# Two convolutions and a spline layer on one core: mask rows laid out channel by channel, the steps' chain moved to GpSimd, one load issued ahead of a store

## The chip, the cores and the metric

The kernel runs on one core of one Trainium2 chip. The metric is the device time of a launch in microseconds; of several runs the median is taken. PE is TensorE, ACT is ScalarE, DVE is VectorE, POOL is GpSimd and SP is SyncE, whose queue issues most of the DMAs.

## The reference

`x` is float32 [32, 64, 56, 56] (32 images, 64 channels). The first block is two 3x3 convolutions, weights reduced to their signs, each followed by a batch norm over images and pixels, a relu between them, and a residual sum. The second block is a spline per channel.

```python
w1b = sign(w1); w2b = sign(w2)
out = relu(_batchnorm(_conv3x3(x, w1b), gamma1, beta1))
out = _batchnorm(_conv3x3(out, w2b), gamma2, beta2)
x   = relu(out + x)
...
x_aff = clip(x * a + b, -CLAMP, CLAMP)
u = (x_aff + 1.0) * 0.5 * (K - 1)
i = floor(u); t = clip(u - i, 0, 1)
spline = alpha_table[i0] * b0 + alpha_table[i1] * b1 + alpha_table[i2] * b2 + alpha_table[i3] * b3
y_nl = einsum('bchwr,cr->bchw', spline, mix)
return id_gain * x + y_nl + bias
```

`K` is 32 knots, `alpha_table` is [32, 8], `mix` is [64, 8], and `b0` to `b3` are the cubic basis functions of `t`.

## The kernel before, in words

**Three stages.** The first convolution reads the 32 images as 16 pairs (128 partitions: 2 images of 64 channels) and stores its result in a scratch tensor; the second reads that, with batch norm and relu applied on the way in, and stores to a second scratch tensor; the spline stage reads that, adds `x`, and works through 32 chunks of 128 x 1568 values. Pairs are counted over both convolutions: 0 to 15 in the first, 16 to 31 in the second.

**A pair of a convolution.** SP loads it (L273 in a loop, L294 for the first two pairs of the second convolution, each of those with two small halo DMAs). In the second convolution ACT normalises it in place (L381) and writes its high part as fp16 (L399); the pair that opens the convolution goes in pieces (L365, L374). DVE normalises the halo (L480 to L492) and writes the low part (L509). PE multiplies all taps, both parts, 288 products in four tiles (L741). ACT evacuates each half (L420), DVE takes statistics (L547), SP stores (L279). Each engine runs its own list in order; the lists are written in rounds of two pairs, with the first and the last round of each convolution written out apart. Where the first convolution ends, SP's list is: store of pair 14, load and halo of pair 16, store of pair 15, load and halo of pair 17 (L288 to L296).

**The tables.** In the first convolution's first round PE multiplies `alpha` with three arrangements of `mix` (L720): as it is, and for each half of the channels repeated for four groups (`mix_by_group`, filled by eight small DMAs, L240). DVE scales the result and makes 17 centres' coefficients of five tables (`coefficients`, L572). In the second convolution's first round DVE forms the differences between neighbouring centres, picks for each partition those of its group and splits them into a high and a low part (`steps`, L599 to L619). GpSimd then writes 80 diagonal weight tiles of 128 x 32 from them (L349), which PE uses only in the spline stage.

**A chunk of the spline stage.** Each channel's value at a pixel has a cell number. Sixteen DMAs (`spread`, L938) copy the chunk's cells into `cell4`, so that four rows of partitions hold the same channel; row `g` of the four is compared with thresholds of its own. Before, those rows are `g * 32 + channel`. Comparing gives four masks: two "middle" masks by DVE (L1161, `middle`) and two "edge" masks by ACT (L1058). PE multiplies the masks with the diagonals into one of two PSUM buffers by turns (L1303), table by table: NEAR and FAR with all four masks, middle ones first, then SQ, LIN and VAL with the edge masks alone; SQ also takes a product that adds the near part (L1313). DVE reads each table: `near_cube` (L1181), `far_cube` (L1188), `square` (L1202), `slope` (L1210), `value` (L1223), and does `far_part` (L1195), `add_slope` (L1216), `finish` (L1230), `offsets` (L1154), `fixed` (L1146), `linear` (L1140) between. A table may be begun when the one two before it has been read. The order on DVE is written by hand (L1276 to L1294). A middle mask of the next chunk may be written when PE has done with the one of this chunk, which is after FAR's middle products; it waits for the whole FAR table (L1160).

The chunk that opens the stage spreads its cells by products with an identity, whose 32 columns are taken four times (L1327), instead of DMAs.

```python
def middle(c, q):
    dve.wait_ge(copied[c % 2], copies(c))
    dve.wait_ge(table_ready, used(c - 1, T_FAR))
...
def table(c, t):
    wait_past(pe, table_used, used(c, t) - 2)
```

## Time and profile before

| what | value |
|---|---|
| median of 3 runs | 1140.85 us (1138.58 to 1143.94) |
| profiled execution, its own time | 1139.08 us |
| its span | 1137.2 us, mean granted clock 0.989 |
| PE busy | 1081.0 us (95%) |
| DVE busy | 966.2 us (85%) |
| ACT busy | 899.3 us (79%) |
| POOL busy | 137.5 us (12%) |
| DMA | 259.46 MB, mean 228 GB/s |

The first convolution lasts until about 204 us of the span, the second until about 411, the spline stage until the end. Busy time is the time in which an engine executes; the difference to the span is idle time, and it only matters on the engine that the others wait for.

### The profile page before, as it was taken

Reading aid. Unit: us, or ns where it says so; the run is one execution under the profiler, and the core shown is the slowest. Engines: PE = TensorE matmul, PEld = TensorE weight load, DVE = VectorE, ACT = ScalarE, POOL = GpSimd, SP = SyncE. Lnnn points to the kernel's source line nnn. Section 1 sums busy time; section 2 is a strip of 40 time slices with the busy share of each in tenths; the row PEclk is TensorE's granted clock in tenths of the full one; section 3 lists DMA queues with packets and bytes.
Section 4 is the critical chain, followed back from the end, with each engine's and each line's share of the span. In section 5 each row is a group of like instructions: output and inputs, shape, how many; then the busy total and the mean of one; then the engine's idle time right before and its main releaser. Section 6 shows DMA issues by size and latency. Waiting matters only on the chain.

```text
span 1137.2 us, 53175 instructions
## 1 busy us (share of the span) xinstructions
PE 1081.0 (95%) x24650; PEld 724.2 (64%) x24650; DVE 966.2 (85%) x959; ACT 899.3 (79%) x410; POOL 137.5 (12%) x195
## 2 busy tenths in 40 slices
PE   6999999699999968999999999999999999999996
PEld 5777777577777745556656656656666556656564
DVE  5856656687767779999999999999999998999997
ACT  4445443767777648999999999999999999999971
POOL 6000000058100000101101011011110110101100
PEclk9999999899999989999999999999999999999999
DMA  8677674677677936799898989989989988998652
GB/s 288 221 293 285 251 278 175 224 248 298 263 284 291 349 164 161 185 233 225 228 234 213 237 203 234 222 220 235 228 209 235 226 225 212 233 233 200 165 131 87
DMA packets 57465, 259.46 MB, mean 228 GB/s; under 512 B 16080, under 2 KB 16080, under 8 KB 49232
## 3 DMA queue, kind: packets, MB, share of 16 engines
q1 hardware_dynamic: 48496, 208.40, 54.6%
q0 software_dynamic: 8640, 48.17, 23.2%
q8 instruction: 148, 2.42, 0.9%
q10 hardware_dynamic: 160, 0.30, 0.1%
q14 instruction: 21, 0.17, 0.0%
HBM read 104.29 MB, written 77.07 MB: 159 GB/s over the span
## 4 chain that ended last, share of the span: by engine, by line
PE 86%; DVE 7%; issue 3%; DMA 1%; ACT 1%; SPq 0%; DVEq 0%; ACTq 0%
PE tab L1303 49%; PE acc L741 30%; PE tab L1313 7%; DVE middle_mask L1161 1%; DMA halo<-y_scratch 1%; DVE far_sq L1210 1%; DMA w_raw<-in_w 1%; ACT xin L381 1%; ACT yout L420 1%; DVE poly L1202 0%; DVE far L1188 0%; DVE stats L547 0%; DVE offset L1154 0%; DVE poly L1216 0%; DVE band_split L509 0%
## 5 line engine op out<-in xcount | busy, mean ns | idle before, releaser
L1303 PE MATMUL tab<-edge_mask,diag 128*32 128x392 bf16 x10240 | 446.6, 329 | 5.8 <-issue 2.5
L1303 PEld LDWEIGHTS tab<-edge_mask,diag 128*32 128x32 f16 x10240 | 283.5, 97 | 160.6 <-issue 20.1
L1058 ACT ACTIVATE edge_mask<-cell,thr 128x6272 bf16<-128x6272 bf16 x62 | 338.6, 5509 | 2.0 <-DMA cell<-cell 2.0
L420 ACT ACTIVATE yout<-acc 128x1568 f32<-128x1568 f32 x64 | 94.5, 1477 | 167.5 <-PE acc L741 146.9
L741 PE MATMUL acc<-band_split,w 64*64 64x385 f16 (+2 forms) x4608 | 194.6, 329 | 9.9 <-DVE band_split L509 4.9
L741 PE MATMUL acc<-split,w 64*64 64x385 f16 (+3 forms) x4608 | 191.5, 326 | 11.2 <-DVE w L468 10.0
L1303 PE MATMUL tab<-middle_mask,diag 128*32 128x392 bf16 x4096 | 187.2, 329 | 7.5 <-issue 5.5
L547 DVE BATCH_NORM_STATS2 stats<-yout 128x392 f32 (+1 forms) x240 | 117.9, 555 | 89.1 <-ACT yout L420 89.1
L741 PEld LDWEIGHTS acc<-band_split,w 64*64 64x64 f16 x4608 | 150.0, 109 | 54.3 <-issue 8.8
L741 PEld LDWEIGHTS acc<-split,w 64*64 64x64 f16 x4608 | 144.7, 108 | 57.1 <-issue 11.9
L1303 PEld LDWEIGHTS tab<-middle_mask,diag 128*32 128x32 f16 x4096 | 110.6, 97 | 72.6 <-DVE middle_mask L1161 10.4
L1161 DVE TENSOR_SCALAR middle_mask<-cell,thr 128x6272 bf16<-128x6272 bf16 x62 | 114.5, 1846 | 0.0
L973 POOL DMA_DIRECT2D lin<-far x32 | 50.2, 1568 | 497.7 <-DVE far L1195 497.7
L1313 PE MATMUL tab<-poly,ident 128*32 128x392 f32 x1024 | 92.4, 493 | 1.3 <-issue 1.3
L1188 DVE SCALAR_TENSOR_TENSOR far<-tab,first,far 128x1568 f32<-128x1568 f32 x31 | 57.4, 1851 | 25.6 <-PE tab L1303 25.6
L520 DVE SCALAR_TENSOR_TENSOR split<-split,xin 128x3136 f16<-128x3136 f16 (+4 forms) x19 | 55.0, 2908 | 10.1 <-ACT split L410 9.8
L1033 ACT ACTIVATE poly<-offset 128x1568 f32<-128x1568 int32 x32 | 48.4, 1511 | 18.6 <-DVE offset L1154 16.9
L1313 PEld LDWEIGHTS tab<-poly,ident 128*32 128x32 f32 x1024 | 34.1, 110 | 43.6 <-issue 38.7
L1202 DVE SCALAR_TENSOR_TENSOR poly<-tab,first,dist_sq 128x1568 f32<-128x1568 f32 x31 | 57.3, 1847 | 4.1 <-PE tab L1313 4.1
L1181 DVE SCALAR_TENSOR_TENSOR poly<-tab,first,poly 128x1568 f32<-128x1568 f32 x31 | 57.2, 1846 | 4.0 <-PE tab L1303 4.0
L1195 DVE SCALAR_TENSOR_TENSOR far<-far,cst,far_sq 128x1568 f32<-128x1568 f32 x32 | 59.3, 1852 | 1.2
L1210 DVE SCALAR_TENSOR_TENSOR far_sq<-tab,first,offset 128x1568 f32<-128x1568 f32 x31 | 57.2, 1846 | 0.9 <-PE tab L1303 0.8
(140 smaller groups left out, 962.0 us busy)
## 6 DMA issues: line engine op xcount, KB each, us to landing
y_scratch<-yout SPq DMA_DIRECT2D x32, 1568.0 KB, 6.2
cell<-cell SPq DMA_DIRECT2D x496, 98.0 KB, 4.6
xin<-y_scratch SPq DMA_DIRECT2D x16, 1568.0 KB, 6.2
lin<-far POOLq DMA_DIRECT2D x32, 784.0 KB, 8.6
out<-lin SPq DMA_DIRECT2D x31, 784.0 KB, 5.3
xin<-in_x SPq DMA_DIRECT2D x15, 1568.0 KB, 6.5
lin<-y_scratch SPq DMA_DIRECT2D x30, 784.0 KB, 9.3
lin<-in_x POOLq DMA_DIRECT2D x28, 784.0 KB, 7.9
```

The source lines that it names most:

```text
L420: act.activation(yout[b][:, :].rearrange("p (r k x) -> p k r x", r=2, k=TILES)[:, 2 * part:2 * part + 2], acc[:, 4 * part:4 * part + 4, 0: ...
L547: dve.bn_stats(stats[:, bass.ds(COUNTS * (g - base) + t, 1), :], yout[b][:, own]).then_inc(counted, 1)
L741: mm = pe.matmul(to[:, top:end, cols], weights[part][own, tap * C:(tap + 1) * C], image[own, first + dy + top:first + dy + end, from_cols] ...
L1058: act.activation(mask_of(c, q)[:, :, :], cell4[c % 2][:, :, :], ACT.Sign, bias=thr[:, q:q + 1]).then_inc(sign_mask_ready, 1)
L1161: dve.tensor_scalar(mask_of(c, q)[:, :, :], cell4[c % 2][:, :, :], thr[:, q:q + 1], None, ALU.is_ge).then_inc(mask_ready, 1)
L1181: dve.scalar_tensor_tensor(out=quarters(poly[c % 2]), in0=summed(c, T_NEAR), scalar=base(c, T_NEAR), in1=quarters(poly[c % 2]), op0=ALU.ad ...
L1188: dve.scalar_tensor_tensor(out=quarters(far[c % 2]), in0=summed(c, T_FAR), scalar=base(c, T_FAR), in1=quarters(far[c % 2]), op0=ALU.add, o ...
L1195: dve.scalar_tensor_tensor(out=far[c % 2][:, :], in0=far[c % 2][:, :], scalar=cc(AMP), in1=far_sq[:, :], op0=ALU.mult, op1=ALU.mult).then_ ...
L1202: dve.scalar_tensor_tensor(out=quarters(poly[c % 2]), in0=summed(c, T_SQ), scalar=base(c, T_SQ), in1=quarters(dist_sq), op0=ALU.add, op1=A ...
L1210: dve.scalar_tensor_tensor(out=quarters(far_sq), in0=summed(c, T_LIN), scalar=base(c, T_LIN), in1=quarters(offset[c % 2]), op0=ALU.add, op ...
L1303: mm = pe.matmul(tab[(c + t) % 2][j * GROUP:(j + 1) * GROUP, sub, 0:SUB], keep["diag"][part][:, j % 2, t, q, :], mask_of(c, q)[:, j, sub * ...
L1313: mm = pe.matmul(tab[(c + T_SQ) % 2][j * GROUP:(j + 1) * GROUP, sub, 0:SUB], keep["ident"][:, j * GROUP:(j + 1) * GROUP], poly[c % 2][:, s ...
```

## The change

1. SP no longer issues the eight DMAs that fill `mix_by_group`; GpSimd fills it by eight copies, and PE waits for them before the tables.
2. Where the first convolution ends, the last store (pair 15) goes behind the load and halo of pair 17.
3. `steps` runs on GpSimd, after `coefficients`, by instructions that treat all 128 partitions alike (of_group selects the own row). The five last instructions of `coefficients` no longer wait for one another. Nothing of `steps` remains in DVE's list.
4. The four rows of a channel are now `4 * channel + g` (copies, diagonals' identity, thresholds, `mix_by_group`).
5. The opening chunk's cells are spread by 16 products of 128 x 128 weights instead of 64 with 32 columns each; the weights lie in the memory of `dist_sq`.
6. DVE's middle masks stand earlier in the chunk: the first behind `finish`, the second behind `far_part`. They wait for FAR's last middle product instead of the whole FAR table.

```diff
-                for g in range(4):
-                    sp.dma_start(mix_by_group[:, half, g * GROUP:(g + 1) * GROUP],
-                                 mix_t[:, half * GROUP:(half + 1) * GROUP]).then_inc(small_loaded, 16)
...
-                    if b == 0 and is_last(n):
-                        store(2 * i + 1, 1)
+                if is_last(n):
+                    store(2 * i + 1, 1)
...
+            def fold(t, width):
+
+                while width > 1:
+                    width //= 2
+                    link(pool.tensor_tensor(t[:, 0:width], t[:, 0:width], t[:, width:2 * width], ALU.add))
+
+            def steps():
+
+                for l in range(3):
+                    link(pool.tensor_tensor(step[:, l, :, :], coef[:, l, :, 1:CENTRES], coef[:, l, :, 0:STEPS],
+                                            ALU.subtract))
+                    signed = step[:, l, :, 0:STEPS:2]
+                    link(pool.tensor_scalar(signed, signed, 0.5, None, ALU.mult))
+                link(pool.tensor_tensor(halves[:, :, :], step[:, 0, :, 0:STEPS // 2:2], step[:, 0, :, STEPS // 2:STEPS:2],
+                                        ALU.add))
+                for width in (2, 1):
+                    link(pool.tensor_tensor(halves[:, :, 0:width], halves[:, :, 0:width], halves[:, :, width:2 * width],
+                                            ALU.add))
+                link(pool.tensor_copy(keep["plain"][:, :], coef[:, 0, :, 0]))
+                link(pool.tensor_tensor(keep["first"][:, :], keep["plain"][:, :], halves[:, :, 0], ALU.add))
+                for half in range(2):
+                    for odd, quads in enumerate((EDGE_QUADS, MIDDLE_QUADS)):
+                        to = dsel[:, half, :, quads[0]:quads[1] + 1]
+                        for g in range(4):
+                            frm = step[:, 1 + half, :, 2 * g + odd:STEPS:8]
+                            if g == 0:
+                                link(pool.tensor_scalar(to, frm, of_group[:, g:g + 1], None, ALU.mult))
+                            else:
+                                link(pool.tensor_scalar(own_step[:, :, :], frm, of_group[:, g:g + 1], None, ALU.mult))
+                                link(pool.tensor_tensor(to, to, own_step[:, :, :], ALU.add))
+                link(pool.tensor_copy(dhi16[:, :, :, :], dsel[:, :, :, :]))
+                link(pool.tensor_copy(dhi[:, :, :, :], dhi16[:, :, :, :]))
+                link(pool.tensor_tensor(dlo[:, :, :, :], dsel[:, :, :, :], dhi[:, :, :, :], ALU.subtract))
...
+            link(pool.memset(keep["spread"][:, :, :], 0.0))
+            link(pool.affine_select(out=keep["spread"][:, :, :], in_=keep["spread"][:, :, :], compare_op=ALU.not_equal,
+                                    fill=1.0, base=0, pattern=[[-1, P], [0, 4]], channel_multiplier=1))
             link(pool.memset(ident4[:, :], 0.0))
...
-                                        base=-g * GROUP, pattern=[[-1, GROUP]], channel_multiplier=1))
+                                        base=-g, pattern=[[-4, GROUP]], channel_multiplier=1))
+            link(pool.memset(turn4[:, :], 0.0))
+            for g in range(1, 4):
+                link(pool.affine_select(out=turn4[:, :], in_=turn4[:, :], compare_op=ALU.not_equal, fill=4.0 * g,
+                                        base=-g, pattern=[[-4, GROUP]], channel_multiplier=1))
+            fold(turn4, GROUP)
+            for q in range(QUADS):
+                lowest = SHIFT + 2 * (step_at(q, 0) + 1)
+                link(pool.tensor_scalar(keep["above"][:, q:q + 1], turn, lowest, None, ALU.add))
+                if q in EDGE_QUADS:
+                    link(pool.tensor_scalar(thr[:, q:q + 1], turn, -1.0, 0.5 - lowest, ALU.mult, ALU.add))
+                else:
+                    link(pool.tensor_scalar(thr[:, q:q + 1], turn, lowest, None, ALU.add))
+            for g in range(4):
+                link(pool.tensor_scalar(of_group[:, g:g + 1], turn, 4.0 * g, None, ALU.is_equal))
...
+            pool.wait_ge(small_loaded, 5 * 16)
+            for half in range(2):
                 for g in range(4):
-                    above = SHIFT + 2 * (step_at(q, g) + 1)
-                    link(pool.memset(thr[g * GROUP:(g + 1) * GROUP, q:q + 1],
-                                     0.5 - above if q in EDGE_QUADS else above))
-                    link(pool.memset(keep["above"][g * GROUP:(g + 1) * GROUP, q:q + 1], above))
-
+                    pool.tensor_copy(mix_by_group[:, half, g:P:4],
+                                     mix_sb[:, half * GROUP:(half + 1) * GROUP]).then_inc(mix_spread, 1)
...
-            pool.wait_ge(steps_ready, 1)
+            pool.wait_ge(coefficients_ready, TABLES)
+            steps()
...
-                    link(dve.tensor_scalar(coef[:, :, t, :], coef[:, :, t, :], f, None, ALU.mult), chain)
-
-            def steps():
...
+                    dve.tensor_scalar(coef[:, :, t, :], coef[:, :, t, :], f, None,
+                                      ALU.mult).then_inc(coefficients_ready, 1)
...
-                    if n == half_rounds:
-                        steps()
...
-                pe.wait_ge(small_loaded, 13 * 16)
+                pe.wait_ge(small_loaded, 5 * 16)
+                pe.wait_ge(mix_spread, 8)
...
-                        sp.dma_start(cell4[c % 2][g * GROUP:(g + 1) * GROUP, j, :],
+                        sp.dma_start(cell4[c % 2][g:P:4, j, :],
...
-                dve.wait_ge(table_ready, used(c - 1, T_FAR))
+                dve.wait_ge(middle_used, c)
...
                 finish(c - 1)
+                if c + 1 < CHUNKS:
+                    middle(c + 1, MIDDLE_QUADS[0])
                 far_cube(c)
                 far_part(c)
                 if c + 1 < CHUNKS:
-                    middle(c + 1, MIDDLE_QUADS[0])
+                    middle(c + 1, MIDDLE_QUADS[1])
                 square(c)
                 if c + 1 < CHUNKS:
                     offsets(c + 1)
                 slope(c)
-                if c + 1 < CHUNKS:
-                    middle(c + 1, MIDDLE_QUADS[1])
                 add_slope(c)
...
-                ones = keep["ident"][:, :].bitcast(BF16)
                 for j in (2 * s, 2 * s + 1):
                     for u in range(2):
-                        for g in range(4):
-                            mm = pe.matmul(tab[s][g * GROUP:(g + 1) * GROUP, 2 * (j % 2) + u, 0:SUB],
-                                           ones[:, 2 * GROUP * j + 1:2 * GROUP * (j + 1):2],
-                                           cell[0][:, (2 * h + u) * SUB:(2 * h + u + 1) * SUB], start=True, stop=True)
+                        mm = pe.matmul(tab[s][:, 2 * (j % 2) + u, 0:SUB],
+                                       keep["spread"][:, j * GROUP:(j + 1) * GROUP, :],
+                                       cell[0][:, (2 * h + u) * SUB:(2 * h + u + 1) * SUB], start=True, stop=True)
...
+                    if t == T_FAR and q == MIDDLE_QUADS[-1]:
+                        mm.then_inc(middle_used, 1)
...
+            "dist_sq": sb("dist_sq", [P, CHUNK]),
...
+        keep["spread"] = keep["dist_sq"][:, 0:2 * P].bitcast(BF16).rearrange("p (k g) -> p k g", g=4)
```

SP's queue at the end of the first convolution, before. The two stores that stand first (x2) are those of pairs 13 and 14; `xin` and `halo` are the loads of a pair and its halo.

```order
L221 REGISTER_ALU
L221 COMPARE_AND_BRANCH
L279 DMA y_scratch<-yout 128x3136 x2
L294 DMA xin<-y_scratch 128x3136
L294 DMA halo<-y_scratch 64x2x56 x2
L279 DMA y_scratch<-yout 128x3136
L294 DMA xin<-y_scratch 128x3136
L294 DMA halo<-y_scratch 64x2x56 x2
L273 DMA xin<-y_scratch 128x3136
```

And now:

```order
L226 REGISTER_ALU
L226 COMPARE_AND_BRANCH
L281 DMA y_scratch<-yout 128x3136 x2
L296 DMA xin<-y_scratch 128x3136
L296 DMA halo<-y_scratch 64x2x56 x2
L296 DMA xin<-y_scratch 128x3136
L296 DMA halo<-y_scratch 64x2x56 x2
L281 DMA y_scratch<-yout 128x3136
L275 DMA xin<-y_scratch 128x3136
```

The store of pair 15 moved behind the load of pair 17 and its halo.

DVE's list in a chunk of the spline stage, before (L1161 are the middle masks, L1188 `far_cube`, L1202 `square`, L1210 `slope`):

```order
L1181 SCALAR_TENSOR_TENSOR poly<-tab,first,poly 128x1568
L1230 SCALAR_TENSOR_TENSOR lin<-poly,cst,lin 128x1568
L1188 SCALAR_TENSOR_TENSOR far<-tab,first,far 128x1568
L1195 SCALAR_TENSOR_TENSOR far<-far,cst,far_sq 128x1568
L1161 TENSOR_SCALAR middle_mask<-cell,thr 128x6272
L1202 SCALAR_TENSOR_TENSOR poly<-tab,first,dist_sq 128x1568
L1154 TENSOR_SCALAR offset<-zbuf 128x1568
L1210 SCALAR_TENSOR_TENSOR far_sq<-tab,first,offset 128x1568
L1161 TENSOR_SCALAR middle_mask<-cell,thr 128x6272
L1216 SCALAR_TENSOR_TENSOR poly<-far_sq,poly 128x1568
```

And now (L1192 are the masks, L1219 `far_cube`, L1233 `square`, L1241 `slope`):

```order
L1212 SCALAR_TENSOR_TENSOR poly<-tab,first,poly 128x1568
L1261 SCALAR_TENSOR_TENSOR lin<-poly,cst,lin 128x1568
L1192 TENSOR_SCALAR middle_mask<-cell,thr 128x6272
L1219 SCALAR_TENSOR_TENSOR far<-tab,first,far 128x1568
L1226 SCALAR_TENSOR_TENSOR far<-far,cst,far_sq 128x1568
L1192 TENSOR_SCALAR middle_mask<-cell,thr 128x6272
L1233 SCALAR_TENSOR_TENSOR poly<-tab,first,dist_sq 128x1568
L1185 TENSOR_SCALAR offset<-zbuf 128x1568
L1241 SCALAR_TENSOR_TENSOR far_sq<-tab,first,offset 128x1568
L1247 SCALAR_TENSOR_TENSOR poly<-far_sq,poly 128x1568
```

The first mask moved from behind `far_part` to ahead of `far_cube`, the second from behind `slope` to ahead of `square`.

## Rows read from the trace of the kernel before

**Rows 1.** Busy time per engine in two stretches: us, count, clock, DMA share, GB/s.

```profile
250.00:380.00 130.00, 128.93 (x3134) 97.25 (x3130) 96.92 (x177) 92.85 (x44) 34.03 (x59) 1.00 0.75 283
...
500.00:700.00 200.00, 196.55 (x4382) 123.10 (x4386) 188.91 (x119) 194.71 (x85) 23.17 (x19) 1.00 0.90 225
```

**Rows 2.** Timeline, opening of the second convolution: start, length, [idle before <- releaser].

```profile
195.41 1.39 SPq L294 DMA_DIRECT2D halo<-y_scratch  x1
...
206.39 0.38 SPq L294 DMA_DIRECT2D xin<-y_scratch  x1
...
217.64 3.00 ACT L381 ACTIVATE xin<-xin,cst 128x3136 f32<-128x3136 f32 x1 [2.47 <-DMA halo<-y_scratch]
...
223.58 3.50 DVE L509 SCALAR_TENSOR_TENSOR band_split<-band_split,xin 128x1568 f16<-128x1568 f16 x2 [4.32 <-ACT band_split L399]
...
227.18 13.79 PE L741 MATMUL acc<-band_split,w 64*64 64x392 f16 x288 [3.37 <-DVE band_split L509]
```

**Rows 3.** Windows of one us: PE, PEld, DVE, ACT, POOL, granted clock, DMA.

```profile
228.00:229.00 1.00, 1.00 (x21) 0.85 (x16) 0.96 (x3) 1.00 (x1) 0.00 (x0) 0.50 1.05 201
...
241.00:242.00 1.00, 0.00 (x0) 0.00 (x0) 1.00 (x1) 0.97 (x1) 1.00 (x1) 1.00 0.00 0
```

**Rows 4.** Timeline, two evacuations one pair apart in the first convolution.

```profile
179.72 1.48 ACT L420 ACTIVATE yout<-acc 128x1568 f32<-128x1568 f32 x1 [4.50 <-PE acc L741]
...
191.54 1.48 ACT L420 ACTIVATE yout<-acc 128x1568 f32<-128x1568 f32 x1 [4.42 <-PE acc L741]
```

**Rows 5.** Timeline around the steps' chain in the second convolution's first round.

```profile
231.09 0.23 DVE L602 TENSOR_TENSOR step<-coef 128x80 f32<-128x80 f32 x1
...
237.07 0.38 POOL L349 TENSOR_SCALAR diag<-ident,dhi 128x32 f16<-128x32 f32 x1 [210.44 <-DVE dlo L618]
...
238.67 3.54 DVE L509 SCALAR_TENSOR_TENSOR band_split<-band_split,xin 128x1568 f16<-128x1568 f16 x2
239.04 3.32 POOL L349 TENSOR_SCALAR diag<-ident,dhi 128x32 f16<-128x32 f32 x1
...
242.47 2.85 PE L741 MATMUL acc<-band_split,w 64*64 64x392 f16 x65 [1.50 <-DVE band_split L509]
```

**Rows 6.** Timeline, a quiet chunk of the spline stage, DVE and PE.

```profile
900.48 1.85 DVE L1188 SCALAR_TENSOR_TENSOR far<-tab,first,far 128x1568 f32<-128x1568 f32 x1 [0.53 <-PE tab L1303]
...
904.14 1.85 DVE L1161 TENSOR_SCALAR middle_mask<-cell,thr 128x6272 bf16<-128x6272 bf16 x1
...
908.54 1.84 DVE L1210 SCALAR_TENSOR_TENSOR far_sq<-tab,first,offset 128x1568 f32<-128x1568 f32 x1
...
910.30 1.84 DVE L1161 TENSOR_SCALAR middle_mask<-cell,thr 128x6272 bf16<-128x6272 bf16 x1
...
910.78 2.93 PE L1303 MATMUL tab<-middle_mask,diag 128*32 128x392 bf16 x64
...
913.54 2.83 PE L1303 MATMUL tab<-edge_mask,diag 128*32 128x392 bf16 x64
...
917.66 1.85 DVE L1181 SCALAR_TENSOR_TENSOR poly<-tab,first,poly 128x1568 f32<-128x1568 f32 x1
...
921.80 1.85 DVE L1188 SCALAR_TENSOR_TENSOR far<-tab,first,far 128x1568 f32<-128x1568 f32 x1 [0.53 <-PE tab L1303]
```

**Rows 7.** Waits of the whole span: us in total, times, longest.

```profile
PE acc L741 <- DVE split L520: 0.5, 1, 0.5
```

**Rows 8.** Timeline of PE from chunk 1 to chunk 2.

```profile
472.13 2.84 PE L1303 MATMUL tab<-edge_mask,diag 128*32 128x392 bf16 x64 [0.81 <-DVE poly L1202]
...
476.54 1.51 PE L1303 MATMUL tab<-middle_mask,diag 128*32 128x392 bf16 x32 [0.24 <-DVE middle_mask L1161]
```

**Rows 9.** DMA view: the cell copies (us to landing), and queue 1 in 429 to 441.

```profile
cell<-cell SPq DMA_DIRECT2D x496, 98.0 KB, 4.6
...
q1 hardware_dynamic: 700, 1.49, 54.2%
```

**Rows 10.** Waits in 480 to 1100 us.

```profile
PE tab L1303 <- issue: 8.0, 7, 2.1
```

32 lines of the change are left out of this document (9 added, 23 removed).

## The prediction

> **What bounds the kernel now.** I read the page's engine totals first (PE is busy 95% of the span), then the windows by stage, the chain of waits for the places where PE stands still, and the timeline around each. In the late part of the second convolution PE is busy 128.93 of 130 us, and in the spline stage 196.55 of 200, beside DVE at 188.91 and ACT at 194.71 [rows 1]. So PE sets the time nearly everywhere, and a change pays only where PE waits. There are three such places that this change touches.
>
> The first is the opening of the second convolution. The load of its second pair (image data of pair 17, counted over both convolutions, and its halo) is issued at 206.39, behind the first convolution's last store [rows 2]. ACT starts to normalise that pair at 217.64, after 2.47 us of waiting for the halo, so it was free at 215.17; DVE's split follows at 223.58, and PE, done with the first pair, stands still for 3.37 us until 227.18 [rows 2]. What follows costs more: after that idle time the granted clock is 0.50 (1.2 GHz) in 228 to 229 [rows 3]. That pair takes PE 13.79 us, where a pair at full clock takes 191.54 - 179.72 = 11.82, read from the distance of two evacuations in the first convolution [rows 2, 4]. A pair later PE waits 1.50 us more, for DVE's split, which began at 238.67 because the steps' chain stood ahead of it, from 231.09 until GpSimd's first diagonal could start at 237.07 [rows 5]; inside that gap of 1.50 us the clock is at 1.00 (2.4 GHz) [rows 3], and no slower stretch follows it.
>
> The second is the change of chunk in the spline stage. In a quiet stretch a chunk lasts 21.32 us (far_cube at 921.80 has one 21.32 before it, at 900.48, and so have the others). The second middle mask starts at 910.30 and ends at 912.14; PE's 64 products with middle masks are busy for 2.93 us from 910.78, the 64 with edge masks after them, from 913.54, for 2.83 [rows 6]. So 0.10 to 0.11 us is lost in a chunk: 2.76 from start to start, where 2.65 would do.
>
> The third is small: a wait of 0.5 us for DVE's split behind the coefficients [rows 7].
>
> **The change part by part.** *The load ahead of the store.* Before, the first pair's halo DMAs are issued from 195.41 for 1.39, so SP is free at 196.80, and its next wait (lo_done) had long been met. The load of pair 17 will go out there, 9.6 us earlier. Today its halo lands by 217.64, 11.2 us after that issue; as long a flight from 196.8 ends at 208, before ACT's 215.17. ACT's two passes, 2.47 us earlier, let DVE start at 223.58 - 2.47 = 221.11, and PE at 227.18 - 2.45 = 224.73, after a gap of 0.92. **Gain 2.45 us.** A gap of 1.50 us did not lower the clock and one of 3.37 did; 0.92 lies below both, so I take the clock as kept, and the pair as 11.82 instead of 13.79: **gain 1.97 us**, with bounds of 0 (the clock falls all the same) and 1.97. The store goes out when it does now, since it waits for ACT's last evacuation; the loads behind it wait for DVE's splits of pair 16, much later. The load queues behind the first pair's load on the same queue, so that one isn't delayed.
>
> *The steps' chain on GpSimd.* DVE loses its chain between the statistics and the next halo, 231.09 to about 237.0, 5.9 us. The split of pair 18, ready today at 238.67 + 3.54 = 242.21, is then ready at 236.3 at the latest. PE will want it at 224.73 + 11.82 = 236.55. **Gain 1.50 us**; bounds 1.50 and, if the split comes a microsecond later, 0.7. On GpSimd the chain is 42 instructions, and 80 for the diagonals as before. A diagonal took 0.38 us [rows 5]; with a link of 0.1 (an estimate) 122 x 0.48 = 59 us, twice that if DVE holds it up. It starts in the first convolution's second round, and PE reads the diagonals in the spline stage, over 25 pairs of 11.8 us later; only if that cover of 300 us were gone would it cost. The diagonal at 239.04 took 3.32 us beside DVE's split, while the two splits together took 3.54, against 3.50 in the pair before [rows 2, 5], so GpSimd was what waited [rows 5]; I cost DVE nothing. The Trainium skill (SBUF — State Buffer, Who interferes with whom) says more: a DVE instruction with two SBUF inputs and a GpSimd one that reads SBUF exclude each other, and the first to start wins, so DVE can lose too. By that rule each of the first convolution's splits could start up to one short GpSimd instruction late; the row agrees for one side only, and the sum would stay the same, since PE isn't waiting for DVE there.
>
> *Coefficients without links.* Five instructions no longer wait for one another; I take 0.3 of the 0.5 us wait [rows 7]. **Gain 0.3 us**, bounds 0 and 0.5.
>
> *Masks earlier on DVE.* Of a chunk's 21.32 us DVE is idle only 0.53, before far_cube [rows 6], so its work is 20.79. PE without its loss needs 21.32 - 0.11 = 21.21, in eight pieces of about 2.65 (NEAR and FAR two each, SQ one and the one that adds the near part, LIN and VAL one each). With both masks where the diff puts them, DVE's one wait per chunk moves to near_cube, 0.30 after NEAR's last product: 5.6 us into the chunk. Steps from the rows: near_cube to far_cube 4.14 less 0.53 idle = 3.6, far_cube (900.48) to mask (904.14) 3.66, mask to slope 4.40 of which the mask 1.76 [rows 6]. So the first mask starts at 5.6 + 3.6 = 9.2 (PE has released the buffer at 7.95), far_cube at 11.0, the second mask at 14.6, square at 16.4 and ends at 18.25, slope at 19.05 and ends at 20.9. PE wants square at 18.55 and slope at 21.2: 0.3 us of slack at either, and the masks are over 4 us early. **Gain 0.11 x 29 chunks = 3.2 us.** But in chunk 1, where DVE is still behind, the second mask now stands before square. There PE's VAL started at 472.13 and the wait for the mask ended at 476.54 [rows 8]. Now VAL starts 1.76 later, at 473.9, NEAR at 473.9 + 2.65 = 476.55 without a mask wait, and its second half, which before started at 476.54, at 477.88: **loss 1.3 us**. Net 1.9; bounds 3.2 and, if the slack of 0.3 proves 0.1 short, -1.
>
> *Rows channel by channel.* Copies, diagonals and thresholds keep number and size; only the destination's partitions are every fourth. The copies take 4.6 us to land [rows 9]. They are issued in the chunk before their use, and no engine waits for them in the chunk shown. I cost this at nothing, either way. The Trainium skill (SBUF — State Buffer, Door 1: The DMA port swizzle) says that 32 neighbouring partitions reach half of the DMA ports; partitions four apart reach all of them on the write side, the read side is unchanged. By that rule the copies get no slower, perhaps faster, which no wait would turn into time.
>
> *The rest.* 16 products of 128 rows replace 64 in column groups of 32 that ran four abreast: the same time within 0.3 us. Eight small DMAs go, and eight GpSimd copies must be done before PE builds the tables behind the second pair's first tile, over 11.8 us after PE began; GpSimd's opening grows by a few short operations. I call it covered; without cover it is a microsecond or two.
>
> **Sum:** 2.45 + 1.97 + 1.50 + 0.3 + 1.9 = 8.1 us. The profiled execution took 1139.08 us, which makes 1131.0. The median of the three runs, 1140.85, is 1.8 above it, so I say 1132.7.
>
> **The rivals.** *A. The clock falls or the second gap comes back* (chance 0.14). For it: 0.92 us is worked out from other engines' times, and pair 18's split has only 0.25 us of slack. Then 8.1 - 1.97 - 1.5 = 4.6, time 1136.2. Against: both gaps shrink by amounts that rows give.
>
> *B. DVE's new order costs what it gains or more* (0.13). DVE is busy 188.91 of 200 us. If square or slope come 0.1 us too late in each chunk, 3 us go and the start's 1.3 remain: gain 8.1 - 3.2 - 3 = 1.9, time 1139. Against: the one idle of 0.53 [rows 6].
>
> *C. The copies get slower* (0.07), the case on the other side. The DMA engines are busy 0.90 of the spline stage [rows 1]. In 429 to 441, with the copies nearly alone, they hold 54.2% of 12 us = 6.5 us in which they moved 1.49 MB [rows 9], so a chunk's 1.57 MB cost 6.9 us of its 0.90 x 21.3 = 19.2. From a copy time 1.3 times today's the engines are full and each chunk waits; at 1.5 times a chunk takes 19.2 + 3.4 = 22.6 us, 1.4 more, over 30 chunks 42 us: 1175. Against: each partition's run is the same 3136 bytes.
>
> *D. PE's unexplained pauses* (within all cases): in the spline stage it stands still for 8.0 us, seven times, with nothing to wait for [rows 10]. They may fall otherwise, by 2 or 3 us.
>
> **How the numbers follow.** My forecast has 0.66: 1132.7, itself within 1128 and 1136. A measurement of this kernel can tell about 0.5%, 5.7 us, from no change, so faster is below 1135.1. Forecast: most of it faster; A and B mostly the same; C slower, with a little of B. Faster 0.67, same 0.24, slower 0.09. The range leaves out C and the tails: 1127 to 1140.
>
> **What would show it.** In the changed profile: the pair-17 load issued near 197, no ACT wait for a halo at 217, PE's gap near 224 under 1 us, the clock at 1.00 from 216 on, the next gap gone, the second convolution's end about 6 us earlier; no wait of the weight load for middle masks, DVE's idle time ahead of near_cube instead of far_cube, and chunks of 21.21 us. Wrong would be: the clock at 0.50 near 228, PE waiting for square or slope, masks or ACT waiting for copies, or an idle PE at 26 us.

## The result and the profile after

The changed kernel took 1126.34 us (median, 1123.17 to 1131.16) against 1139.11 for the kernel before: ratio 0.9883, 95% interval 0.985 to 0.9916, so 12.8 us or 1.2% faster. Three repeats beside the experiments gave 0.99, 0.988 and 0.9896, gains of 11.7, 12.6 and 10.9 us. One execution among all runs, of the kernel b_steps below, took 1919.33 us and is left out of its numbers. I had forecast 1132.7 us, a gain of 8.1, and a range that began at 1127: the direction and most places were right, the size too small.

The profiled execution took 1126.34 us, its span 1124.5, 12.7 less than before. First the opening of the second convolution, in the timeline of the changed kernel (start, length, engine and line, in brackets the idle time before and what ended it):

```profile
197.69 0.87 SPq L296 DMA_DIRECT2D xin<-y_scratch  x1
...
210.72 14.30 PE L771 MATMUL acc<-band_split,w 64*64 64x392 f16 x288 [3.61 <-DVE band_split L540]
...
216.17 2.99 ACT L433 ACTIVATE xin<-xin,cst 128x3136 f32<-128x3136 f32 x1
...
222.10 3.49 DVE L561 SCALAR_TENSOR_TENSOR band_split<-band_split,xin 128x1568 f16<-128x1568 f16 x2 [2.39 <-ACT band_split L451]
...
225.70 30.32 PE L771 MATMUL acc<-band_split,w 64*64 64x392 f16 x728 [0.68 <-issue]
...
233.94 3.49 DVE L561 SCALAR_TENSOR_TENSOR band_split<-band_split,xin 128x1568 f16<-128x1568 f16 x2
```

The load of pair 17 goes out at 197.69 instead of 206.39 [rows 2], ACT normalises that pair without a wait, and PE stands still for 0.68 us instead of 3.37. From 225.70 it then works through 30.32 us: the gap of 1.50 us before pair 18 [rows 5] is gone, since DVE's split of that pair starts at 233.94. The windows (busy us of PE, PEld, DVE, ACT and POOL, granted clock, DMA share, GB/s) show the clock, and the later stretch of [rows 1]:

```profile
500.00:700.00 200.00, 199.13 (x4513) 133.85 (x4505) 195.19 (x122) 198.38 (x84) 24.74 (x18) 1.00 0.88 229
228.00:229.00 1.00, 1.00 (x32) 0.83 (x25) 0.00 (x0) 1.00 (x2) 0.00 (x0) 1.00 0.94 401
```

The clock stays at 1.00 in 228 to 229, where it was 0.50 [rows 3]. In 500 to 700 PE stands still for 0.87 us instead of 3.45, at a DMA share of 0.88 instead of 0.90. How long the second convolution lasts is read from the start of its first pair to the matmul that averages the statistics behind it. In the kernel before, the PE timeline has them at

```profile
209.63 14.18 PE L741 MATMUL acc<-band_split,w 64*64 64x392 f16 x288 [3.60 <-DVE band_split L488]
...
412.87 0.38 PE L813 MATMUL acc<-mv,avg 128*128 128x2 f32 x2 [2.33 <-DVE mv L656]
```

and in the changed one the second of them at

```profile
408.63 0.38 PE L843 MATMUL acc<-mv,avg 128*128 128x2 f32 x2 [2.33 <-DVE mv L687]
```

so 412.87 - 209.63 = 203.24 us have become 408.63 - 210.72 = 197.91. The start itself lies 1.1 us later than before (210.72 against 209.63); in the eighteen traces it lies anywhere from 209.6 to 212.3, for the kernel before and its variants too, so this is not put down to the change.

GpSimd now makes the steps in the first convolution, from the same timeline:

```profile
45.90 3.42 POOL L324 TENSOR_TENSOR step<-coef 128x80 f32<-128x80 f32 x1 [16.19 <-DVE coef L649]
...
54.45 3.33 POOL L344 TENSOR_TENSOR dsel<-dsel,own_step 128x10 f32<-128x10 f32 x1
...
70.47 0.38 POOL L401 TENSOR_SCALAR diag<-ident,dhi 128x32 f16<-128x32 f32 x1
```

Its chain takes 24.6 us, most links 0.2 to 0.35 us and three over 3.3. Here is a quiet chunk (one in which PE never waits), DVE and PE:

```profile
1029.79 2.84 PE L1334 MATMUL tab<-middle_mask,diag 128*32 128x392 bf16 x64
...
1035.40 1.85 DVE L1212 SCALAR_TENSOR_TENSOR poly<-tab,first,poly 128x1568 f32<-128x1568 f32 x1 [0.27 <-PE tab L1334]
...
1038.93 1.85 DVE L1192 TENSOR_SCALAR middle_mask<-cell,thr 128x6272 bf16<-128x6272 bf16 x1
1040.70 1.85 DVE L1219 SCALAR_TENSOR_TENSOR far<-tab,first,far 128x1568 f32<-128x1568 f32 x1
...
1044.36 1.85 DVE L1192 TENSOR_SCALAR middle_mask<-cell,thr 128x6272 bf16<-128x6272 bf16 x1
...
1046.12 1.85 DVE L1233 SCALAR_TENSOR_TENSOR poly<-tab,first,dist_sq 128x1568 f32<-128x1568 f32 x1
...
1048.77 1.85 DVE L1241 SCALAR_TENSOR_TENSOR far_sq<-tab,first,offset 128x1568 f32<-128x1568 f32 x1
...
1050.99 2.32 PE L1334 MATMUL tab<-middle_mask,diag 128*32 128x392 bf16 x49
```

The next chunk's masks are done well ahead, DVE's one wait stands at near_cube, and the chunk lasts 1050.99 - 1029.79 = 21.20 us, where it was 21.32 [rows 6]. Chunk 1 pays for it:

```profile
465.94 1.85 DVE L1192 TENSOR_SCALAR middle_mask<-cell,thr 128x6272 bf16<-128x6272 bf16 x1
467.71 1.85 DVE L1233 SCALAR_TENSOR_TENSOR poly<-tab,first,dist_sq 128x1568 f32<-128x1568 f32 x1
...
469.61 2.84 PE L1334 MATMUL tab<-edge_mask,diag 128*32 128x392 bf16 x64 [2.57 <-DVE poly L1233]
...
476.85 1.84 PE L1334 MATMUL tab<-edge_mask,diag 128*32 128x392 bf16 x40 [0.75 <-issue]
```

The second mask stands before square, and PE waits 2.57 us for square (0.81 before [rows 8]). Here the clock stayed at 1.00 behind that wait. It did not always: nine traces have this wait of 2.57 us, and in five of them (again, again2, old_rows, old_rows2 and few_copies, described below) the clock was at 0.50 (1.2 GHz) for about 3 us behind it, as in the first repeat:

```profile
468.41 4.37 PE L1334 MATMUL tab<-edge_mask,diag 128*32 128x392 bf16 x64 [2.57 <-DVE poly L1233]
```

```profile
469.00:470.00 1.00, 1.00 (x16) 0.49 (x12) 1.00 (x2) 1.00 (x1) 0.00 (x0) 0.50 0.92 185
```

From the near part's add in chunk 1 to that in chunk 2 it is 22.63 us before, 24.0 to 24.9 where the clock held, and 25.5 where it fell. Last the waits and the DMA view of the changed kernel: PE's waits for nothing in 500 to 1100 (in total, times, longest), the copies of the cells (KB, us to landing), and queue 1 in 425 to 437, where the first copies run nearly alone (packets, MB, share):

```profile
PE tab L1334 <- issue: 3.5, 6, 1.2
```

```profile
cell<-cell SPq DMA_DIRECT2D x496, 98.0 KB, 4.0
...
q1 hardware_dynamic: 704, 1.49, 47.6%
```

PE's pauses "<- issue" fell from 8.0 us [rows 10] to 3.5. The copies land after 4.0 us instead of 4.6, and for 1.49 MB they hold the DMA engines for 0.476 x 12 = 5.7 us instead of 6.5 [rows 9].

From here on a measure is used that every trace gives: the distance between the starts of the add of the near part (the 32 matmuls tab<-poly,ident) in chunk 2 and in chunk 31, less 29 times a quiet chunk. It is what PE's **pauses** cost in 29 chunks, with the rare wait beside them and the slower clock behind some of them. Before, 488.49 to 1120.07 is 631.58 us, less 29 x 21.31 leaves 13.6. After, 486.46 to 1107.37 is 620.91, less 29 x 21.20 leaves 6.1. So of the 12.7 us of span, 5.3 come from the second convolution, 3.2 from the quiet chunks and 7.5 from shorter pauses; 2.3 are lost in chunk 1 (0.75 of them a pause) and 1.1 ahead of the second convolution. The 7.5 were not in the forecast.

### The profile page after: what moved, and what is told of

It reads as the page before. It is cut to its first block, busy times and chain, and to the rows that moved or that the text cites. A ratio compares the mean times of both kernels' runs of the same rounds, so it can differ in the third digit from the quotient of the medians.

```text
span 1124.5 us, 53088 instructions
## 1 busy us (share of the span) xinstructions
PE 1074.4 (96%) x24602; PEld 751.0 (67%) x24602; DVE 963.5 (86%) x931; ACT 899.2 (80%) x410; POOL 170.2 (15%) x236
## 4 chain that ended last, share of the span: by engine, by line
PE 94%; DVE 3%; issue 1%; DMA 1%; ACT 0%; ACTq 0%; DVEq 0%
PE tab L1334 52%; PE acc L771 34%; PE tab L1344 8%; DMA w_raw<-in_w 1%; DVE middle_mask L1192 0%; DVE far_sq L1241 0%; PE tab L1356 0%; DVE poly L1233 0%; DVE lin L1276 0%; DVE poly L1272 0%; DVE middle_mask L1201 0%; DVE stats L581 0%; ACT zbuf L1044 0%; DVE edge_mask L1201 0%; DVE offset L1185 0%
## 5 line engine op out<-in xcount | busy, mean ns | idle before, releaser
L1334 PE MATMUL tab<-edge_mask,diag 128*32 128x392 bf16 x10240 | 453.0, 329 | 9.7 <-issue 4.3
L1334 PEld LDWEIGHTS tab<-edge_mask,diag 128*32 128x32 f16 x10240 | 297.5, 97 | 153.5 <-issue 16.3
L771 PE MATMUL acc<-split,w 64*64 64x385 f16 (+3 forms) x4608 | 192.2, 327 | 11.5 <-DVE w L520 10.3
L771 PE MATMUL acc<-band_split,w 64*64 64x385 f16 (+3 forms) x4608 | 192.7, 327 | 6.5 <-DVE band_split L540 3.6
L771 PEld LDWEIGHTS acc<-split,w 64*64 64x64 f16 x4608 | 143.9, 108 | 59.0 <-issue 12.8
L1334 PEld LDWEIGHTS tab<-middle_mask,diag 128*32 128x32 f16 x4096 | 119.2, 97 | 56.7 <-issue 2.4
L1192 DVE TENSOR_SCALAR middle_mask<-cell,thr 128x6272 bf16<-128x6272 bf16 x62 | 114.6, 1848 | 0.0
L999 POOL DMA_DIRECT2D lin<-in_x x28 | 32.3, 1153 | 257.7 <-ACT lin L1016 257.7
L1344 PEld LDWEIGHTS tab<-poly,ident 128*32 128x32 f32 x1024 | 46.1, 110 | 29.8 <-issue 16.5
L572 DVE SCALAR_TENSOR_TENSOR split<-split,xin 128x3136 f16<-128x3136 f16 (+4 forms) x19 | 55.0, 2907 | 10.1 <-ACT split L462 10.0
L1233 DVE SCALAR_TENSOR_TENSOR poly<-tab,first,dist_sq 128x1568 f32<-128x1568 f32 x31 | 57.3, 1848 | 3.8 <-PE tab L1344 3.6
L1219 DVE SCALAR_TENSOR_TENSOR far<-tab,first,far 128x1568 f32<-128x1568 f32 x31 | 57.4, 1851 | 2.1 <-PE tab L1334 1.7
L1064 ACT ACTIVATE poly<-offset 128x1568 f32<-128x1568 int32 x32 | 48.4, 1513 | 12.7 <-DVE offset L1185 12.4
```

The costliest lines, as they stand in the source:

```text
L572: dve.scalar_tensor_tensor(out=inner(split[b][1], first, end), in0=inner(split[b][0], first, end), scalar=-SPLIT, in1=rows(xin[b], first, ...
L771: mm = pe.matmul(to[:, top:end, cols], weights[part][own, tap * C:(tap + 1) * C], image[own, first + dy + top:first + dy + end, from_cols] ...
L1192: dve.tensor_scalar(mask_of(c, q)[:, :, :], cell4[c % 2][:, :, :], thr[:, q:q + 1], None, ALU.is_ge).then_inc(mask_ready, 1)
L1219: dve.scalar_tensor_tensor(out=quarters(far[c % 2]), in0=summed(c, T_FAR), scalar=base(c, T_FAR), in1=quarters(far[c % 2]), op0=ALU.add, o ...
L1233: dve.scalar_tensor_tensor(out=quarters(poly[c % 2]), in0=summed(c, T_SQ), scalar=base(c, T_SQ), in1=quarters(dist_sq), op0=ALU.add, op1=A ...
L1334: mm = pe.matmul(tab[(c + t) % 2][j * GROUP:(j + 1) * GROUP, sub, 0:SUB], keep["diag"][part][:, j % 2, t, q, :], mask_of(c, q)[:, j, sub * ...
```

## The experiments

Sixteen runs followed, some of them repeats. Names that begin with b_ are the kernel before with one edit, the others the changed kernel with one or two edits. The table gives the median, the ratio to the kernel before with its interval, the length of the second convolution as above, the quiet chunk, the pauses, and the DMA share in 500 to 1100, the last four from the one trace of each.

| kernel | us | ratio (95%) | 2nd conv. | quiet | pauses | DMA |
|---|---|---|---|---|---|---|
| before | 1139.11 | 1 | 203.24 | 21.31 | 13.6 | 0.88 |
| changed | 1126.34 | 0.9883 (0.985 to 0.9916) | 197.91 | 21.20 | 6.1 | 0.84 |
| again | 1127.48 | 0.99 (0.9876 to 0.9925) | 197.08 | 21.20 | 6.7 | 0.84 |
| again2 | 1125.96 | 0.988 (0.9843 to 0.9916) | 196.83 | 21.20 | 6.4 | 0.84 |
| again3 | 1127.40 | 0.9896 (0.9867 to 0.9925) | 197.38 | 21.20 | 6.2 | 0.84 |
| old_rows | 1128.64 | 0.9904 (0.9883 to 0.9925) | 196.84 | 21.20 | 17.1 | 0.88 |
| old_rows2 | 1130.36 | 0.9915 (0.9882 to 0.9948) | 197.55 | 21.20 | 10.3 | 0.89 |
| old_masks | 1127.20 | 0.989 (0.9866 to 0.9913) | 196.91 | 21.31 | 7.9 | 0.84 |
| old_rows_masks | 1131.38 | 0.9931 (0.9907 to 0.9956) | 197.09 | 21.31 | 12.5 | 0.88 |
| old_load | 1129.44 | 0.9914 (0.9895 to 0.9933) | 201.20 | 21.20 | 5.7 | 0.84 |
| rows_steps | 1133.30 | 0.9942 (0.991 to 0.9975) | 201.29 | 21.31 | 8.2 | 0.84 |
| b_steps | 1134.41 | 0.9961 (0.994 to 0.9982) | 201.61 | 21.31 | 9.5 | 0.88 |
| b_masks | 1140.52 | 1.0022 (1.0 to 1.0043) | 203.37 | 21.20 | 12.5 | 0.89 |
| b_load | 1139.24 | 0.9997 (0.998 to 1.0015) | 203.25 | 21.31 | 12.4 | 0.89 |
| b_few_copies | 1132.73 | 0.9951 (0.9934 to 0.9968) | 203.94 | 21.31 | 4.4 | 0.68 |
| few_copies | 1126.13 | 0.9887 (0.9848 to 0.9926) | 197.69 | 21.20 | 4.3 | 0.68 |
| late_chunk1 | 1125.37 | 0.988 (0.9861 to 0.99) | 197.49 | 21.20 | 5.3 | 0.84 |
| late_chunk1b | 1127.38 | 0.9888 (0.9858 to 0.9918) | 198.39 | 21.20 | 10.1 | 0.84 |

Runs of one chip, to be compared by medians: again, old_rows, old_masks, old_load (before 1139.22); b_few_copies, old_rows_masks, late_chunk1, b_masks (1138.7); again2, old_rows2, rows_steps, b_steps (1138.53); b_load, few_copies, late_chunk1b, again3 (1138.31).

### Is it chance: the changed kernel again

> The changed kernel once more. About 7 us of its gain were not in the forecast; they lie in the spline stage, where PE's pauses without a cause shrank (the chunks after chunk 2 took 10.67 us less, 3.2 of it forecast). If that was the chance of one profiled execution, this one should show chunks 2 to 31 several microseconds longer than 620.9 us, or the ratio to the kernel before should rise from 0.988 to about 0.993. If it belongs to the change, chunks 2 to 31 take 620 to 622 us again and the ratio stays at 0.988.

Chunks 2 to 31 took 621.49 us and the ratio was 0.99. The short pauses belong to the change.

### The rows undone

```diff
-                                        base=-g, pattern=[[-4, GROUP]], channel_multiplier=1))
+                                        base=-g * GROUP, pattern=[[-1, GROUP]], channel_multiplier=1))
...
-                    pool.tensor_copy(mix_by_group[:, half, g:P:4],
+                    pool.tensor_copy(mix_by_group[:, half, g * GROUP:(g + 1) * GROUP],
...
-                        sp.dma_start(cell4[c % 2][g:P:4, j, :],
+                        sp.dma_start(cell4[c % 2][g * GROUP:(g + 1) * GROUP, j, :],
```

(and the same reordering in the table that the opening products spread with; the number and size of all operations stay).

> Everything of the change but the rows: the copies of the cells go to 32 neighbouring partitions as before. Theory one (the copies hold the DMA engines less with rows channel by channel, and PE's pauses shrink with that): about 6 to 7 us slower than the changed kernel, quiet chunks still 21.21 us, but the pauses of the spline stage back at 12 to 14 us over the quiet chunks, copies 4.6 us from issue to landing. Theory two (the order of the masks shrank the pauses): as fast as the changed kernel within 2 us, pauses of about 6 us.

The copies took 4.8 us and the pauses were 17.1, but that trace came from the slowest execution, at 1137.23 us; the median was 1.2 us above that of again, inside theory two's 2 us. The two readings disagree, so it ran once more.

> The change with the old rows once more, since its trace (pauses of 17.1 us) came from its slowest execution and its median lay only 1.2 us above the changed kernel's. Theory one (rows free the DMA engines, pauses shrink by 6 us): 3 to 6 us slower than the changed kernel. If the rows are worth about a microsecond and the trace was an outlier: within 2 us, pauses of 8 us.

This time 4.4 us slower than again2 on the same chip (1130.36 - 1125.96), pauses 10.3, copies 4.9 us (again2 took 1125.96 us, with pauses of 6.4 us, as expected of it below). That is theory one's range for the time, and less than its size for the pauses. Its DMA share and PE's pauses in 500 to 1100:

```profile
500.00:1100.00 600.00, 592.21 (x13351) 422.79 (x13346) 577.54 (x360) 583.80 (x246) 74.60 (x54) 1.00 0.89 218
```

```profile
PE tab L1334 <- issue: 7.8, 10, 1.7
```

and those of again2, which differs from it in the rows alone:

```profile
500.00:1100.00 600.00, 597.05 (x13447) 448.75 (x13442) 579.65 (x361) 585.92 (x247) 73.83 (x53) 1.00 0.84 219
```

```profile
PE tab L1334 <- issue: 2.0, 5, 0.7
```

### The masks' order undone, and done alone

```diff
+                far_cube(c)
+                far_part(c)
                 if c + 1 < CHUNKS:
                     middle(c + 1, MIDDLE_QUADS[0])
-                far_cube(c)
-                far_part(c)
-                if c + 1 < CHUNKS:
-                    middle(c + 1, MIDDLE_QUADS[1])
                 square(c)
...
                 slope(c)
+                if c + 1 < CHUNKS:
+                    middle(c + 1, MIDDLE_QUADS[1])
                 add_slope(c)
```

> The change with the masks' old order on DVE (the wait on the middle masks' own semaphore stays). Theory one: quiet chunks 21.32 instead of 21.21 (3.2 us lost over 29 chunks), the 2.3 us that chunk 1 lost are back, pauses stay at about 6 us: 1 us slower than the changed kernel. Theory two: the pauses grow to about 13 us as well: 8 us slower than the changed kernel.

Theory one's case: 21.31 us a chunk, pauses 7.9, time 0.3 us below again, which no measurement here tells from zero. The order of the masks is not what shortened the pauses. The converse, the new order in the kernel before:

> The kernel before with the new order of the masks alone (and the middle masks' own semaphore). By my terms: quiet chunks 21.20 instead of 21.31 (3.2 us gained) less 2.3 us in chunk 1, so 0.9 us faster than before. If the masks' order shortens PE's pauses by itself, the pauses fall from 13.6 to about 8 us and the kernel is 6 us faster than before.

The pauses stayed at 12.5 us, the quiet chunks fell to 21.20, and the kernel was not faster: 1.0022, at best 0, where I had 0.9 us. That answers for the pauses as the first expectation had it; of the 3.2 us in the quiet chunks nothing came out as time.

### The copies thinned out

```diff
         def copies(c):

-            return 256 * (c // 2 + c % 2)
+            return 64 * (c // 2) + 256 * (c % 2)
...
-                for turn in range(4):
+                for turn in range(4 if c == 1 else 1):
```

> The kernel before with a fourth of the copies of the cells from chunk 2 on (4 DMAs of 98 KB a chunk instead of 16; the other three quarters of the masks are made from an older chunk's cells). Nothing else in the engines' work changes. Theory one (PE's pauses come from busy DMA engines, through which its instructions also come): the DMA engines' share in the spline stage falls from 0.90 to about 0.65, and the pauses over the quiet chunks fall from 13.6 us to under 5 us, so the kernel is 8 us or more faster than before. Theory two (the pauses have to do with PE's own instructions or the order of waits): pauses stay at 10 us or more, and the time within 3 us of before.

This kernel leaves out three quarters of the copies, and three quarters of its masks are made of old cells; only its time is of use. Theory one held for the pauses (4.4 us, DMA share 0.68); the time fell by 6.0 us (1138.7 to 1132.73), less than the 8 I had asked for. Nothing was changed here but the number of transfers and the count that is waited for. The kernel's rows in 500 to 1100:

```profile
500.00:1100.00 600.00, 598.35 (x13428) 365.93 (x13424) 577.51 (x363) 588.42 (x249) 67.98 (x54) 1.00 0.68 164
```

```profile
PE tab L1303 <- issue: 1.1, 5, 0.3
```

One pause of the kernel before shows what goes on. In its PE timeline and its windows:

```profile
826.56 1.51 PE L1303 MATMUL tab<-middle_mask,diag 128*32 128x392 bf16 x32 [2.15 <-issue]
```

```profile
824.00:825.00 1.00, 0.41 (x12) 0.11 (x5) 1.00 (x2) 1.00 (x1) 0.00 (x0) 1.00 0.95 280
825.00:826.00 1.00, 0.00 (x0) 0.00 (x0) 0.98 (x1) 1.00 (x2) 0.00 (x0) 1.00 1.02 389
826.00:827.00 1.00, 0.44 (x12) 0.34 (x15) 0.98 (x1) 1.00 (x2) 0.00 (x0) 1.00 0.89 367
827.00:828.00 1.00, 1.00 (x32) 0.73 (x27) 1.00 (x2) 1.00 (x1) 0.83 (x1) 1.00 0.16 48
```

and in its DMA view of 824 to 827 (queue and kind: packets, MB, share of the engines):

```profile
q1 hardware_dynamic: 263, 1.02, 93.1%
q8 instruction: 1, 0.02, 2.1%
```

While the DMA engines are full, PE executes nothing, and one packet of the instruction queue (q8) goes through. It lies in 824.1 to 825.2, whose DMA view has

```profile
q8 instruction: 1, 0.02, 5.8%
```

and there is none in 825.2 to 826.6. PE is back at 826.56, 1.4 us after the packet's end. Nearly every pause looks like this. The eighteen traces have 142 places in 480 to 1100 us where two starts of PE's matmuls lie over 0.5 us apart, and by the packets' own times 139 of them end 1.0 to 1.7 us after the end of an instruction packet. With a packet every 5.8 us, chance would put some 17 there. Places of over 1.5 us are found 20 times in the seven traces with the old rows, 5 times in the nine with the new rows, and never in the two with few copies. The packets themselves take about 1 us in all of them (median 1.04 before, 0.97 in b_few_copies), so it must be their start that comes late; that part is inferred. Over 500 to 1100 the kernel before has

```profile
q8 instruction: 104, 1.70, 1.2%
```

104 packets of 16 KB, in which PE executed 13224 matmuls and 13228 weight loads by the windows, some 250 instructions a packet. That is a packet every 5.8 us, and PE stood still seven times for 8.0 us in all [rows 10]. The Trainium skill (Runtime: NRT & Kernel Launch, Instruction fetch mechanics) has instructions fetched by DMA in 16 KiB blocks of 256 instructions, and calls the cost of crossing a block mostly hidden. The trace agrees with the block; most of the cost is hidden at a DMA share of 0.68, and less of it at 0.88.

The same edit in the changed kernel:

> The changed kernel with a fourth of the cells' copies from chunk 2 on (the other three quarters of the masks come from an older chunk's cells). With old rows the same edit took the pauses from 13.6 to 4.4 us and 6.0 us off the time. If the new rows act through the DMA engines' load too, they have taken part of that already: pauses from 6.4 to about 4.4 us and 2 to 3 us faster than the changed kernel. If the rows act in another way, the edit takes its 6 us again.

(It leaves out the same copies.) Pauses 4.3 us, the same floor as with the old rows, and 1.3 us faster than again3 (1127.4 to 1126.13), which is below the 2 to 3 I had expected and no more than repeats of one kernel differ by. The edit takes 6.0 us where the rows are old and at most this where they are new: the two do not add, so the rows work through the load of the DMA engines as well.

### Both parts in the spline stage undone

> The change without its two parts in the spline stage (old rows and the masks' old order; the load, the steps on GpSimd and the opening products stay). Alone, undoing the rows cost 1.2 us and undoing the masks' order -0.3 us. If the two add up, this is 1 us slower than the changed kernel, 1128.5 us. If either of them is enough to keep the pauses short, both undone give back all that the forecast did not have: quiet chunks 21.31, pauses of about 13 us, and 1134 to 1136 us, the gain left being my terms for the second convolution, 6 us.

(The diffs of old_rows and old_masks together.) 7.3 us faster than before, 4.7 less than old_masks was, with pauses of 12.5. The time lies midway between the two expectations, the pauses at the second. The reading that either part is enough falls with b_masks and old_rows2, whose pauses were long with the new order of the masks.

With the load's old place too, two kernels that differ in the rows alone (rows_steps is old_masks and old_load together, b_steps has old_rows as well):

> The change with the masks' old order and the old place of the load: what is left is the rows, the steps on GpSimd and the opening products. Gaps before pairs 17 and 18 of 3 us and under 0.7 us. With the rows worth 5 us and the steps 1.5 us: 6.5 us faster than the kernel before, quiet chunks 21.31, pauses of 5 to 8 us. Without a worth of the rows: 1.5 us faster.

> The same with the old rows as well: only the steps on GpSimd, the coefficients without links, the opening products of 128 rows and their tiles are left of the change. By my terms 1.5 + 0.3 us faster than the kernel before, pauses of 12 to 14 us, quiet chunks 21.31. The distance from the run before it is the rows' worth: 5 us by theory one, about 1 us by the medians so far.

They were 5.2 and 4.1 us faster than before: the rows are worth 1.1 us here, the lower of the two sizes, and pauses of 8.2 and 9.5 us are close together. The steps and what goes with them gave 4.1 us, more than twice my 1.8; the interval, 2.0 to 6.8 us, begins just above that.

Taken together, the nine traces with new rows and all copies have pauses of 5.3 to 10.1 us, mean 7.0; the seven with old rows 9.5 to 17.1, mean 12.6. The four distances by medians are 1.2, 4.4, 1.1 and 4.7 us, mean 2.9. By the scatter of the executions each has a standard error of 1.5 to 1.9 us, so the two small ones are not told from zero alone; their mean, with an error of 0.8, is. Three of the seven traces with old rows also have a pause behind which the clock fell (old_rows, old_rows_masks, b_load), and none with new rows has; here the one of old_rows:

```profile
801.88 0.84 PE L1334 MATMUL tab<-middle_mask,diag 128*32 128x392 bf16 x15 [2.39 <-issue]
```

```profile
804.00:805.00 1.00, 1.00 (x20) 0.53 (x16) 0.00 (x0) 1.00 (x2) 0.00 (x0) 0.50 0.90 151
```

### The load alone, and the load undone

```diff
-                    if b == 0 and is_last(n):
-                        store(2 * i + 1, 1)
+                if is_last(n):
+                    store(2 * i + 1, 1)
```

> The kernel before with the load of pair 17 ahead of the last store, alone. My terms priced the parts as if each stood by itself: 2.45 us (gap) and 1.97 us (clock), 4.4 us faster. But with the steps' chain still on DVE, the split of pair 18 is ready near 242.2, and PE, which now wants it at 236.6, waits up to 5.6 us. Then either nearly the whole gain of the load goes into that second gap, and after so long a gap the clock falls there instead: within 1 us of before; or, if pair 18's work moves up with the load, the gap stays near 1.5 us: 4 us faster.

The first case, exactly: ratio 0.9997. The PE timeline and two windows of this kernel:

```profile
227.31 12.01 PE L741 MATMUL acc<-band_split,w 64*64 64x392 f16 x288 [0.61 <-issue]
244.99 164.58 PE L741 MATMUL acc<-band_split,w 64*64 64x392 f16 x3954 [5.67 <-DVE band_split L509]
```

```profile
228.00:229.00 1.00, 1.00 (x32) 0.88 (x27) 1.00 (x3) 1.00 (x1) 0.00 (x0) 1.00 0.97 188
...
245.00:246.00 1.00, 1.00 (x16) 0.80 (x20) 1.00 (x3) 0.00 (x0) 0.81 (x3) 0.50 0.96 176
```

The first gap went and the clock held, and both came back a pair later: 5.67 us, and the clock at 0.50 behind it. The second convolution lasts 203.25 us, as before (203.24).

> The change with the load of pair 17 behind the first convolution's last store again. By my terms it loses 2.45 us (the gap before pair 17 back at 3.4 us) and 1.97 us (clock at 0.50 after it, pair 17 at 13.8 us), and keeps the 1.5 us of the second gap: 4.4 us slower than the changed kernel, 8.4 us faster than the kernel before. If clock and gap are not tied, pair 17 takes 11.8 us behind the long gap and only 2.5 us are lost.

2.0 us slower than again by medians, 3.9 in the length of the second convolution (201.20 against a mean of 197.3 in the four traces of the changed kernel). Its gap is 2.3 us longer than their mean of 0.65; the rest of the 3.9 is not traced. The gap and the window behind it:

```profile
227.81 9.50 PE L771 MATMUL acc<-band_split,w 64*64 64x392 f16 x224 [2.98 <-DVE band_split L561]
```

```profile
228.00:229.00 1.00, 1.00 (x31) 0.97 (x27) 1.00 (x3) 1.00 (x2) 0.00 (x0) 1.00 0.68 151
```

The clock held behind 2.98 us, so this is the second of the two cases, whose 2.5 us the medians bear out. In rows_steps, with the same opening, it fell behind 3.07:

```profile
228.85 16.18 PE L771 MATMUL acc<-band_split,w 64*64 64x392 f16 x349 [3.07 <-DVE band_split L561]
```

```profile
230.00:231.00 1.00, 1.00 (x20) 0.71 (x16) 0.63 (x2) 1.00 (x2) 0.00 (x0) 0.50 0.74 201
```

### The loss in chunk 1 taken back

```diff
-                if c + 1 < CHUNKS:
+                if c + 1 < CHUNKS and c > 1:
                     middle(c + 1, MIDDLE_QUADS[0])
                 far_cube(c)
                 far_part(c)
                 if c + 1 < CHUNKS:
-                    middle(c + 1, MIDDLE_QUADS[1])
+                    middle(c + 1, MIDDLE_QUADS[0 if c == 1 else 1])
...
                 slope(c)
+                if c == 1:
+                    middle(c + 1, MIDDLE_QUADS[1])
                 add_slope(c)
```

> The changed kernel with the old order of the masks in chunk 1 alone, where DVE is still behind. Chunk 1 to 2 took 24.89 us with the new order, 22.63 with the old one: 2.2 us faster than the changed kernel, about 1125 us, with the quiet chunks at 21.20 as before. If the loss only moves to chunk 2 (whose table then waits for its mask), chunk 2 to 3 takes over 23 us and the time is the changed kernel's.

Its PE timeline, where VAL of chunk 1 and of chunk 2 begins:

```profile
467.65 2.84 PE L1336 MATMUL tab<-edge_mask,diag 128*32 128x392 bf16 x64 [0.81 <-DVE poly L1233]
...
490.11 2.84 PE L1336 MATMUL tab<-edge_mask,diag 128*32 128x392 bf16 x64 [0.61 <-DVE poly L1233]
```

Chunk 1 to 2 took 22.64 us, but in chunk 2 PE now waits for square, and chunk 2 to 3 took 22.02 instead of 21.20: of the 1.5 us had back, 0.8 moved on (they stand among the 5.3 of the table). The median was 1125.37. It was repeated beside the changed kernel:

> The changed kernel with the masks' old order in chunk 1, once more, beside the changed kernel on the same chip: its trace had chunk 1 to 2 at 22.64 us instead of 25.5, so about 2.5 us faster than the changed kernel.

> The changed kernel a third time, as the partner of the next three on one chip. Its median stood at 0.988 and 0.990 of the kernel before; 0.989 here, pauses of the spline stage 5 to 8 us (6.1 and 6.7 in its two traces).

> The changed kernel as the partner of the three others: 1126 to 1127.5 us as in its earlier medians.

late_chunk1b took 1127.38 us, again3 1127.40. Its trace had chunk 1 to 2 at 23.32 and pauses of 10.1. Chunk 1 to 2 is 24.12 us in again3, whose trace has no pause there, and 22.64 in late_chunk1; with the 0.8 moved on, 0.7 us remain, and 2.1 against the executions in which the clock falls (25.5). Both are less than the pauses vary by from one execution to the next, and no gain is shown. No version here is measurably faster than the changed kernel.

## Why the prediction was wrong

The forecast lay 6.4 us above the measured 1126.34. Of that 1.7 is the kernel before: the median of three, 1140.85, from which I counted, is 1139.11 over the five runs of the result. The other 4.7 is gain that the sum did not have. The miss of the range is only 0.7 us, and two of the three repeats (1127.48 and 1127.40) lie inside it; the size of the gain was wrong in all four.

*The load and the clock* (2.45 and 1.97 us): right. The gap before pair 17 is 0.68 us (forecast 0.92), the clock stays at 1.00, the next pair starts without a wait. *The steps* (1.50): right, the second gap is gone, and in none of the eleven traces with the new place of the load and the steps on GpSimd does PE wait for DVE there, though in the changed kernel's trace the split ends at 237.43 and PE wants it at 225.70 + 11.82 = 237.52. The three terms together were 5.92 us of the second convolution; measured are 5.3 in this trace, 5.9 in the mean of four. But their split into parts was wrong in one point: alone, the load is worth nothing (b_load), since the next pair's split still stood behind the steps' chain. I had written down when that split is ready (242.2) and when PE would want it (236.55), and priced the steps at the 1.50 us of the gap that the trace shows. Behind the earlier load they are worth all of it: 203.25 us with the load alone, 197.3 with both.

*The coefficients* (0.3): not resolved. PE's wait of 0.5 us is gone from the trace, and no run tells so little from zero.

*The masks* (1.9): the mechanism is right to 0.1 us. DVE's steps stood at 5.6, 9.2, 11.0, 14.6, 16.4 and 19.05 us of the chunk in the forecast; in the trace, counted from 1029.79, they start at 5.61, 9.14, 10.91, 14.57, 16.33 and 18.98, and the quiet chunk is 21.20 long (21.21). The loss in chunk 1 is 1.5 us instead of 1.3 where the clock holds: PE waits 1.76 us longer for square and saves the mask's 0.24. Where the clock falls behind that wait it is 2.9 us (25.5 less 22.63), which the prediction did not think of and which leaves of the 3.2 us next to nothing. The net worth by medians is uncertain: the new order was 0.3 and 1.8 us slower in two comparisons (old_masks, b_masks) and, each against its own kernel before, 4.6 us faster from rows_steps to old_load and 0.9 and 3.3 from old_rows_masks to the two runs of old_rows.

***The rows* (0 us, "I cost this at nothing, either way"): this step failed.** The Trainium skill (SBUF — State Buffer, Door 1: The DMA port swizzle) ties a transfer's bandwidth to the number of SBUF ports that its partitions reach. The trace agrees in direction: landing 4.6 to 4.0 us, share of the engines in the spline stage 0.88 to 0.84. I then wrote "which no wait would turn into time". That looked at the engines that wait for the copies, not at what else goes through the same DMA engines. PE's own instructions do, and they were late in the pauses that I had listed as unexplained. With new rows these cost 7.0 us instead of 12.6 in the mean of the traces; by medians the rows are worth 1.1 to 4.7 us.

*The pauses*: rival D had the place and the wrong price. "They may fall otherwise, by 2 or 3 us" was a guess about noise; 7.5 us in the profiled pair was more than any term of the sum. Two rows that I had quoted belonged together: DMA engines busy for 0.90 of the stretch [rows 1], and an engine that stands still for 8.0 us with nothing to wait for [rows 10]. Their upper bound was the whole 8.0, and the range should have reached down by it, to 1132.7 - 8.0 = 1124.7.

*The rest*: the opening products and the tiles behind the first pair cost nothing that shows. Rival A did not come in the changed kernel, but both of its parts came in b_load. Rival B did not come: DVE's only regular idle time is at near_cube, 0.27 us, and no wait of PE for square or slope follows chunk 1. Rival C had the sign wrong.

The sum as it now stands: 5.9 (second convolution) + 3.2 (quiet chunks) - 1.5 (chunk 1) + 5.6 (pauses, by traces) = 13.2 us, or 10.5 with the 2.9 us by medians, each 1.4 less where the clock falls in chunk 1; measured were 10.9 to 12.8. **Open** is why the medians give the rows only about half of what the pauses in the traces show: each kernel has one trace, and pauses differ between executions (6.2 and 10.1 us with the same rows). Open is too where the other 2.3 us of b_steps come from, if they are there; its one trace has pauses 4.1 us shorter than the kernel before's. And it is not shown what makes one instruction packet late and the next one not.

## What to carry to other kernels

A pause in which an engine waits for nothing is a term like any other: put beside it what the DMA engines carry at that moment, and if they are full, count its whole length among what a lighter transfer can give back. "Nobody waits for this transfer" is not enough to cost it at zero; an instruction stream shares the engines. And where two edits clear two stalls in a row, price them together and each alone: the first alone may only push its gain into the second.

## What the runs showed that I had not expected

- Thinning out the copies, with no instruction of PE changed, took PE's pauses from 13.6 to 4.4 us and 6.0 us off the time; some 4 us remain at a DMA share of 0.68.
- PE comes back from a pause 1.0 to 1.7 us after an instruction packet has ended, in 139 of 142 cases.
- The same 98 KB copies with the same runs per partition land in 4.0 us instead of 4.6 when their rows are four partitions apart, and hold the engines for 5.7 us instead of 6.5 for 1.49 MB.
- The length of a gap alone does not tell what the clock does. It was at 0.50 behind idle times of 2.02 us (b_load, at 568), 2.21 (old_rows_masks, at 883), 2.39, 2.57 (five traces), 3.07, 3.37 and 5.67, and it held at 1.00 behind 2.15 (the kernel before, at 826), 2.57 (four traces), 2.98 (old_load) and 2.96, here in b_masks:

```profile
654.51 1.34 PE L1304 MATMUL tab<-middle_mask,diag 128*32 128x392 bf16 x28 [2.96 <-issue]
```
- GpSimd's links of 0.2 to 0.35 us took 3.3 to 3.6 us three times beside DVE's splits of 3.4, as the diagonal had done in [rows 5]; the chain of 24.6 us delayed nothing.
